# Two interleaved accumulation groups in place of two consecutive ones: the order of the map matmuls in a pre-activation directional convolution

## The chip, the cores and the metric

One Trainium2 chip, one of its cores. The metric is the device time of one execution in microseconds (us). The kernel before was run three times: median 2257.04 us, 2256.22 to 2261.09. The trace is of a further, profiled execution of it, which took 2258.2 us; its span, from the first instruction to the last, is 2256.4 us.

## The reference

The input x is 16 images of 256 channels of 56 by 56, float32. What is computed, cut to what matters:

```python
v = group_norm(x)                       # 32 groups of 8 channels, no affine part
h = depthwise_conv3x3(v, dw_weight)     # zero padding
h = gelu(h)
maps = einsum('bchw,oc->bohw', h, pw_weight) + pw_bias   # o: 8 directions x 256 channels
out = 0
for i, (dx, dy) in enumerate(OFFSETS8):
    out += maps[:, i] * (roll(v, (dy, dx)) - v)
return x + out
```

## The kernel before, in words

**Tiling.** An image is cut into seven tiles of eight rows, 448 pixels; 256 channels are two halves of 128 partitions. There are 112 tiles in all, in eight bodies of two images (14 tiles) each, every body written out by the same code; `n0 + nl` is the number of a tile and t its place in its image, 0 to 6. Eight directional maps of two channel halves are needed per tile. The kernel joins two directions to a pair (`PAIRS`), so a tile has eight units, u0 to u7, each of one pair (u divided by two) and one channel half (the remainder). A unit has two sides, one map of 128 by 448 each.

**TensorE.** `make_maps` (L897) makes one unit. Weights and h are split into a high and a low part, so one side is six matmuls of 448 columns that accumulate in one PSUM bank: high and low weights with the high part of h for both halves of the 256 inputs (four), then the high weights with the low part of h (two). A unit is thus 12 matmuls and a tile 96. Each matmul has weights of its own, loaded just ahead of it. The units rotate through three groups of two banks (`GROUPS`, L64), side 0 in the first bank and side 1 in the second; before the first matmul of a unit TensorE waits until VectorE has done with the unit that used the group last (L904, usually three units ago). At the end of a body the order of the groups is changed, so that u6 of tile 13 of a body waits for u4, two units ago. The last matmul of each side counts up `maps_s`.

**ScalarE.** `add_bias` (L584) waits for side 0 of a unit, scales and shifts it in place, then waits for side 1 and does the same. Its stream is in order, and between the units stand its other steps (L622 to L638): after u1 the GELU of tile nl+2 (L577) and the first tap of the convolution of step nl+3 (L567, or L563 in two halves), after u2 the high part of h (L582), after u7 the normalising of tile nl+4 (L548); measuring the next image's moments and copying its edges are placed behind units 3 to 6.

**VectorE.** In order (L852 to L891): the products of u0 and u1 with the field differences (L707, kept as the tile's sums), tap 0, the product of u2 (in place in its PSUM banks), tap 1, the addition of u2 to the sums (L729, which also frees the banks of u2), the product of u3, tap 2, the products of u4 to u7 with taps 3 to 7 between them. The eight taps (L787, or L778 in two halves) belong to the convolution three tiles ahead. `product` waits for both biased sides of its unit (L706), tap 0 for ScalarE's first tap. Where t is 2, the ten short steps of the group statistics (L643) are begun, one at a time between the others, and most of them fall in the tile with t = 3; in that tile the taps are in two halves too.

**GpSimd and the DMA queues.** GpSimd makes the field differences, the low part of h (L340) and three additions of products per tile (L371), and sends the sums with accumulating transfers on its own queue. The SyncE queue loads the images.

Of the kernel before, what the change touches and what calls it, by code (L numbers as in the profile page):

```python
# [5 lines left out]
def preact_directional_conv(nc, x, pw_t, pw_b, dw, out):  # L6
# [4 lines left out]
    P = 128  # L11
    B, C, H, W = x.shape
    HALVES = C // P
# [53 lines left out]
    def last_user(q):  # L67

        p = q - 1
        while GROUPS[p % UNITS_BODY] != GROUPS[q]:  # L70
            p -= 1
        return p
# [6 lines left out]
    with ctx:  # L79
        def sb(name, shape, dt=F32):  # L80
            return ctx.enter_context(nc.sbuf_tensor(name, shape, dt))

        def sem(name):
            return ctx.enter_context(nc.semaphore(name))
# [9 lines left out]
        hhi = sb("hhi", [P, H_SLOTS, 2, PX], F32R)  # L94
        hlo = sb("hlo", [P, H_SLOTS, 2, PX], F32R)
# [20 lines left out]
        w_hi = sb("w_hi", [P, HALVES, DIRS * C], F32R)  # L116
        w_lo = sb("w_lo", [P, HALVES, DIRS * C], F32R)
# [37 lines left out]
        def maps(q):  # L155
            b = 2 * GROUPS[q % UNITS_BODY]
            return psum[:, b:b + 2, 0:PX]

        def unit_map(u, side):

            k, g = divmod(u, HALVES)
            return PAIRS[k][side], g
# [21 lines left out]
        def h_part(h, t, nl, kk):  # L184


            base = nl - t
            if t == TILES - 1:
                return h[:, H_SLOT[base + SINGLE], kk, :]
            return h[:, H_SLOT[base + 2 * (t // 2) + kk], t % 2, :]  # L190
# [27 lines left out]
        hlo_s = sem("hlo_s")  # L218
        maps_s = sem("maps_s")
# [43 lines left out]
        def run(body):  # L263

            for i in range(BODIES):
                body(i * STEPS, i * 2, i == BODIES - 1)
# [628 lines left out]
        @block.tensor  # L895
        def _(pe):
            def make_maps(n0, nl, u):  # L897

                t, q = nl % TILES, nl * UNITS + u

                need = nl + (1 if t == TILES - 1 else 2)
                wanted = t % 2 == 0

                pe.wait_ge(prod_s, n0 * UNITS + (last_user(q) + 1 + PROD0))  # L904
                if u == 0 and wanted:
                    pe.wait_ge(hhi_s, n0 + need)
                for side in range(2):
                    d, g = unit_map(u, side)
                    col = d * C + g * P
                    steps = [(w, hhi, kk) for kk in range(HALVES) for w in (w_hi, w_lo)]  # L910
                    steps += [(w_hi, hlo, kk) for kk in range(HALVES)]
                    for s, (w, h, kk) in enumerate(steps):
                        if u == 0 and side == 0 and s == 2 * HALVES and wanted:
                            pe.wait_ge(hlo_s, n0 + need)
                        last = nc.tensor.matmul(maps(q)[:, side, :], w[:, kk, col:col + P], h_part(h, t, nl, kk),  # L915
                                                start=s == 0, stop=s == len(steps) - 1)
                    last.then_inc(maps_s, 1)

            pe.wait_ge(w_lo_s, 1)

            def body(n0, b0, last):
                for nl in range(STEPS):
                    for u in range(UNITS):
                        make_maps(n0, nl, u)

            run(body)
# [26 lines left out]
```

## Time and profile before

| | |
|---|---|
| median of three runs | 2257.04 us |
| profiled execution | 2258.2 us |
| its span | 2256.4 us, 28684 instructions |
| mean granted TensorE clock | 0.999 of full speed |
| first matmul starts | at 45.4 us |
| last matmul starts | at 2249.5 us |
| TensorE matmul busy | 2194.2 us, 10752 matmuls |
| VectorE busy | 2055.0 us |
| ScalarE busy | 1842.0 us |
| GpSimd busy | 1977.0 us |

The busy time of matmuls is that of overlapping instructions, merged: a row of 0.36 us stands for one matmul, though the next starts 0.20 us after it. The starts are therefore what is to be read of TensorE. Times in the timeline are from the start of the span; "[0.50 <-PE psum L915]" at the end of a row is idle time of that engine ahead of the row, and what ended it. "xN" in a timeline row is N instructions of one kind that follow each other, merged, and its second number is the time from the start of the first to the end of the last.

### The profile page before, as it was taken

To read this page: it belongs to the slowest core of one execution; us is meant where nothing else is said; L and a number is where in the kernel's file an instruction comes from. 1 tells how busy PE (TensorE), PEld (TensorE's weight loads), DVE (VectorE), ACT (ScalarE), POOL (GpSimd) and SP (SyncE) were. 2 spreads that over 40 slices of the span, in tenths; PEclk is the share of its full clock that TensorE was granted. 3 is DMA by queue.
4 is the path that set the end of the run, shared out by engine and by line. 5 is a ranking of instruction groups with operands and counts; after the bars stand their busy time and mean duration, and the time that the engine had idled before them with its cause. 6 is when DMAs were issued, how large, how long until landed. Compare 5 with 4: busy or idle time off the path is not lost.

```text
span 2256.4 us, 28684 instructions
## 1 busy us (share of the span) xinstructions
PE 2194.2 (97%) x10752; PEld 2009.3 (89%) x10752; DVE 2055.0 (91%) x2234; ACT 1842.0 (82%) x2762; POOL 1977.0 (88%) x857
## 2 busy tenths in 40 slices
PE   1999999999999999999999999999999999999998
PEld 1999989999999999999989999999999999999997
DVE  7999989999899999999989999899999999989995
ACT  5978888788887888889788887888878888787775
POOL 5889888899988998899898988989888998889985
PEclk9999999999999999999999999999999999999999
DMA  6245263443725337164452644526354372543414
GB/s 180 50 83 117 50 112 93 90 99 52 156 47 106 90 58 156 33 108 97 74 131 35 122 94 82 112 50 129 76 93 96 61 159 34 107 98 50 98 33 74
DMA packets 47083, 202.13 MB, mean 90 GB/s; under 512 B 3040, under 2 KB 7136, under 8 KB 45664
## 3 DMA queue, kind: packets, MB, share of 16 engines
q0 software_dynamic: 30192, 94.97, 25.8%
q1 hardware_dynamic: 16752, 105.34, 18.2%
q8 instruction: 84, 1.38, 0.2%
q14 instruction: 55, 0.45, 0.1%
HBM read 104.88 MB, written 146.80 MB: 112 GB/s over the span
## 4 chain that ended last, share of the span: by engine, by line
PE 89%; DVE 5%; ACT 4%; issue 2%; DMA 0%; POOL 0%; SPq 0%; ACTq 0%; DVEq 0%
PE psum L915 89%; DVE psum L707 1%; ACT psum L592 1%; DVE psum L787 1%; ACT hid L577 1%; ACT psum L563 1%; DVE acc L729 1%; DVE products L707 1%; DVE psum L778 1%; DMA acc<-x 0%; ACT psum L567 0%; DVE acc L759 0%; POOL hlo L340 0%; DVE fields L810 0%; DVE part_sums L797 0%
## 5 line engine op out<-in xcount | busy, mean ns | idle before, releaser
L592 ACT ACTIVATE psum<-psum,bias,rstd 128x448 f32<-128x448 f32 x1792 | 1203.7, 694 | 373.8 <-PE psum L915 369.7
L915 PE MATMUL psum<-hhi,w_hi 128*128 128x448 f32 x3584 | 1315.0, 367 | 55.4 <-ACT hhi L582 45.4
L371 POOL TENSOR_TENSOR acc<-acc,products 128x896 f32<-128x896 f32 x333 | 1165.1, 3499 | 231.4 <-DVE products L707 224.9
L915 PE MATMUL psum<-hhi,w_lo 128*128 128x448 f32 x3584 | 1305.3, 364 | 0.0
L915 PE MATMUL psum<-hlo,w_hi 128*128 128x448 f32 x3584 | 1014.1, 364 | 0.3 <-POOL hlo L340 0.3
L787 DVE SCALAR_TENSOR_TENSOR psum<-xn,dw_f,psum 128x896 f32<-128x896 f32 x768 | 881.2, 1148 | 79.8 <-ACT psum L567 76.3
L915 PEld LDWEIGHTS psum<-hhi,w_hi 128*128 128x128 f32 x3584 | 672.5, 188 | 137.8 <-issue 45.4
L915 PEld LDWEIGHTS psum<-hlo,w_hi 128*128 128x128 f32 x3584 | 672.5, 188 | 52.4 <-POOL hlo L340 0.9
L915 PEld LDWEIGHTS psum<-hhi,w_lo 128*128 128x128 f32 x3584 | 672.9, 188 | 50.0
L707 DVE TENSOR_TENSOR products<-psum,fields 128x896 f32<-128x896 f32 x555 | 600.9, 1083 | 37.9 <-ACT psum L592 35.6
L707 DVE TENSOR_TENSOR acc<-psum,fields 128x896 f32<-128x896 f32 x224 | 241.2, 1086 | 46.3 <-ACT psum L592 44.7
L340 POOL TENSOR_TENSOR hlo<-hid,hhi 128x896 fp32r<-128x896 f32 x112 | 264.6, 2363 | 12.7 <-ACT hhi L582 12.7
L356 POOL TENSOR_TENSOR fields<-xpad 128x896 f32<-128x896 f32 (+1 forms) x112 | 240.1, 2144 | 0.0
L352 POOL TENSOR_TENSOR fields<-xpad 128x912 f32<-128x912 f32 (+1 forms) x112 | 210.1, 1876 | 0.0
L778 DVE SCALAR_TENSOR_TENSOR psum<-xn,dw_f,psum 128x448 f32<-128x448 f32 x256 | 160.7, 677 | 6.5 <-ACT psum L563 6.5
L707 DVE TENSOR_TENSOR psum<-psum,fields 128x896 f32<-128x896 f32 x117 | 128.6, 1099 | 17.7 <-ACT psum L592 10.7
L378 POOL DMA_DIRECT2D out<-acc x111 | 132.7, 1196 | 7.8 <-DMA out<-acc 7.2
L729 DVE TENSOR_TENSOR acc<-psum,acc 128x896 f32<-128x896 f32 x111 | 120.1, 1082 | 0.2
L548 ACT ACTIVATE xn<-xpad,shift,rstd 128x1008 f32<-128x1008 f32 (+1 forms) x96 | 116.5, 1214 | 0.0
L577 ACT ACTIVATE hid<-psum 128x896 f32<-128x896 f32 x112 | 102.0, 911 | 12.0 <-DVE psum L787 12.0
L567 ACT ACTIVATE psum<-xn,dw_f 128x896 f32<-128x896 f32 x96 | 97.5, 1016 | 9.0 <-ACT hid L577 0.4
L582 ACT CAST hhi<-hid 128x896 fp32r<-128x896 f32 x112 | 104.8, 936 | 0.0
(67 smaller groups left out, 447.9 us busy)
## 6 DMA issues: line engine op xcount, KB each, us to landing
out<-acc POOLq DMA_DIRECT2D x96, 896.0 KB, 7.7
out<-x SPq DMA_DIRECT2D x16, 3136.0 KB, 12.9
xpad<-x SPq DMA_DIRECT2D x30, 1568.0 KB, 15.2
out<-acc POOLq DMA_DIRECT2D x15, 448.0 KB, 5.7
acc<-x SPq DMA_DIRECT2D x4, 784.0 KB, 6.9
xpad<-pw_t SPq DMA_DIRECT2D x1, 2048.0 KB, 12.3
out<-products SPq DMA_DIRECT2D x2, 224.0 KB, 1.9
dw_f<-dw SPq DMA_DIRECT2D x1, 9.0 KB, 8.2
```

The costliest lines, as they stand in the source:

```text
L340: nc.gpsimd.tensor_tensor(hlo[:, slot], hid[:], hhi[:, slot].bitcast(F32), ALU.subtract).then_inc(hlo_s, 1)
L352: nc.gpsimd.tensor_tensor(gx[:, :, f + 2 * lo:f + TR, :], v[:, :, r + 2 * lo:r + TR, 1:WP], v[:, :, r + 2 * lo:r + TR, 0:WP - 1], ALU.subt ...
L356: nc.gpsimd.tensor_tensor(gy[:, :, f + lo:f + ROWS + 1, :], v[:, :, r + lo + 1:r + TR, 1:W + 1], v[:, :, r + lo:r + ROWS + 1, 1:W + 1], AL ...
L371: nc.gpsimd.tensor_tensor(a, a, p, ALU.add).then_inc(added_s, 1)
L378: pool.dma_start(out_dst[b, :, :, t * PX:(t + width) * PX], acc[buf][:, :, sign].rearrange("p g t x -> p g (t x)"), accum_op=ALU.add).then ...
L577: nc.scalar.activation(hid[:], conv_of(n0, c), ACT.Gelu).then_inc(gelu_s, 1)
L592: nc.scalar.activation(m, m, ACT.Identity, bias=bias[ip][:, g, d:d + 1], scale=rstd[ip][:, g:g + 1]).then_inc(biased_s, 1)
L707: return nc.vector.tensor_tensor(to.rearrange("p s (r c) -> p s r c", c=W), maps(q).rearrange("p s (r c) -> p s r c", c=W), field, ALU.mult)
L729: nc.vector.tensor_tensor(a, maps(nl * UNITS + u), a, ALU.add).then_inc(prod_s, 1)
L778: nc.vector.scalar_tensor_tensor(d, xn[c % 2][:, g * TR + ky:g * TR + ky + ROWS, kx:kx + W], dw_f[:, g, TAPS_DVE[j]:TAPS_DVE[j] + 1], d, A ...
L787: nc.vector.scalar_tensor_tensor(d, xn[c % 2][:, ky:ky + 2 * ROWS, kx:kx + W].rearrange("p (a r) c -> p a r c", a=2), dw_f[:, g, TAPS_DVE[ ...
L915: last = nc.tensor.matmul(maps(q)[:, side, :], w[:, kk, col:col + P], h_part(h, t, nl, kk), start=s == 0, stop=s == len(steps) - 1)
```

## The change

For each unit, the loop over the six steps now stands outside and the loop over the two sides inside. Matmul s of side 0 is followed by matmul s of side 1, each into its own bank; the weights, the moving operands, the number of matmuls and of weight loads, the order of the units, the rotation of the groups and the wait ahead of a unit stay. The wait for the low part of h in u0 stands ahead of the first of the four matmuls that read it, so it now has eight matmuls before it and not four. The counts of `maps_s` come at the last two matmuls of the unit. No other engine's code is changed.

```diff
-                for side in range(2):
-                    d, g = unit_map(u, side)
-                    col = d * C + g * P
-                    steps = [(w, hhi, kk) for kk in range(HALVES) for w in (w_hi, w_lo)]
-                    steps += [(w_hi, hlo, kk) for kk in range(HALVES)]
-                    for s, (w, h, kk) in enumerate(steps):
-                        if u == 0 and side == 0 and s == 2 * HALVES and wanted:
-                            pe.wait_ge(hlo_s, n0 + need)
+                steps = [(w, hhi, kk) for kk in range(HALVES) for w in (w_hi, w_lo)]
+                steps += [(w_hi, hlo, kk) for kk in range(HALVES)]
+                for s, (w, h, kk) in enumerate(steps):
+                    if u == 0 and s == 2 * HALVES and wanted:
+                        pe.wait_ge(hlo_s, n0 + need)
+                    for side in range(2):
+                        d, g = unit_map(u, side)
+                        col = d * C + g * P
                         last = nc.tensor.matmul(maps(q)[:, side, :], w[:, kk, col:col + P], h_part(h, t, nl, kk),
                                                 start=s == 0, stop=s == len(steps) - 1)
-                    last.then_inc(maps_s, 1)
+                        if s == len(steps) - 1:
+                            last.then_inc(maps_s, 1)
```

## Rows read from the trace of the kernel before

**Rows 1.** The page: busy time (share of the span) and instructions of each engine.

```profile
PE 2194.2 (97%) x10752; PEld 2009.3 (89%) x10752; DVE 2055.0 (91%) x2234; ACT 1842.0 (82%) x2762; POOL 1977.0 (88%) x857
```

**Rows 2.** Who waited for whom: us in total, times, longest.

```profile
ACT psum L592 <- PE psum L915: 369.7, 711, 2.2
...
PEld psum L915 <- DVE acc L729: 33.4, 83, 0.8
...
PE psum L915 <- DVE acc L729: 6.1, 16, 0.5
...
PE psum L915 <- POOL hlo L340: 0.3, 1, 0.3
```

**Rows 3.** Timeline of TensorE's matmuls in one tile: start, us, instructions.

```profile
1094.38 0.56 PE L915 MATMUL psum<-hlo,w_hi 128*128 128x448 f32 x2
1094.78 0.36 PE L915 MATMUL psum<-hhi,w_hi 128*128 128x448 f32 x1
...
1101.58 0.56 PE L915 MATMUL psum<-hlo,w_hi 128*128 128x448 f32 x2
...
1102.09 0.48 PE L915 MATMUL psum<-hhi,w_hi 128*128 128x448 f32 x1
...
1102.40 0.37 PE L915 MATMUL psum<-hhi,w_lo 128*128 128x448 f32 x1
```

**Rows 4.** Timeline of ScalarE in the same stretch.

```profile
1094.98 0.70 ACT L592 ACTIVATE psum<-psum,bias,rstd 128x448 f32<-128x448 f32 x1 [0.50 <-PE psum L915]
1095.60 0.91 ACT L577 ACTIVATE hid<-psum 128x896 f32<-128x896 f32 x1
1096.61 1.02 ACT L567 ACTIVATE psum<-xn,dw_f 128x896 f32<-128x896 f32 x1
1097.56 1.30 ACT L592 ACTIVATE psum<-psum,bias,rstd 128x448 f32<-128x448 f32 x2
1098.78 0.94 ACT L582 CAST hhi<-hid 128x896 fp32r<-128x896 f32 x1
```

**Rows 5.** Timeline of VectorE in the same stretch.

```profile
1094.97 2.08 DVE L707 TENSOR_TENSOR acc<-psum,fields 128x896 f32<-128x896 f32 x2
1097.66 1.16 DVE L787 SCALAR_TENSOR_TENSOR psum<-xn,dw_f,psum 128x896 f32<-128x896 f32 x1 [0.60 <-ACT psum L567]
1098.89 1.10 DVE L707 TENSOR_TENSOR psum<-psum,fields 128x896 f32<-128x896 f32 x1
1099.90 1.15 DVE L787 SCALAR_TENSOR_TENSOR psum<-xn,dw_f,psum 128x896 f32<-128x896 f32 x1
1100.95 1.08 DVE L729 TENSOR_TENSOR acc<-psum,acc 128x896 f32<-128x896 f32 x1
```

**Rows 6.** Stretches of time: length, PE busy (matmuls), granted clock, DMA share, GB/s.

```profile
67.58:2190.46 2122.88, 2114.24 (x10369) 1.00 0.44 88
1089.98:1109.42 19.44, 19.44 (x97) 1.00 0.29 48
1169.27:1189.09 19.82, 19.82 (x97) 1.00 0.25 80
106.43:126.36 19.93, 19.48 (x98) 1.00 0.28 47
2034.22:2054.15 19.93, 19.48 (x98) 1.00 0.28 47
1679.92:1700.00 20.08, 19.70 (x98) 1.00 0.70 132
2190.46:2209.66 19.20, 19.20 (x97) 1.00 0.29 49
```

**Rows 7.** Timeline of TensorE behind two waits: the first and the last slow start.

```profile
138.77 0.36 PE L915 MATMUL psum<-hhi,w_lo 128*128 128x448 f32 x1
138.98 0.37 PE L915 MATMUL psum<-hhi,w_hi 128*128 128x448 f32 x1
...
1947.78 0.37 PE L915 MATMUL psum<-hhi,w_lo 128*128 128x448 f32 x1
1947.99 0.57 PE L915 MATMUL psum<-hlo,w_hi 128*128 128x448 f32 x2
```

**Rows 8.** Line L915: duration in ns, least, median and most, and first and last start.

```profile
L915 PEld LDWEIGHTS psum<-hhi,w_hi x3584: 186/188/330, 45.4 to 2248.7; 128*128 128x128 f32 x200
```

## The prediction

> **What bounds the kernel now.** The page's first part comes first: matmuls cover 97% of the span, and no other engine is above 91% [rows 1]. TensorE looks like the bound, but matmuls overlap, so I went on to the starts. From the first matmul of tile 1 to that of tile 109 are 2122.88 us, 108 tiles, 19.66 us a tile; one of the last tiles, where VectorE has no taps left to do, takes 19.20 us, which is 96 steps of 0.200 us [rows 6]. So a tile holds 0.46 us that the matmul stream alone doesn't need. The list of waits says where some of it goes: TensorE waits for the addition of u2 (L729) in 83 + 16 = 99 tiles [rows 2]. That wait is short, but its frequency is what matters: in 99 of 111 tiles the banks of u2 come free later than u5 would like to start. The timelines of one such tile show the path that decides it. Call M the start of the last matmul of u1's side 1, 1094.58 (the second of the pair at 1094.38) [rows 3]. ScalarE, idle for 0.50 us, starts the bias of that side 0.40 us later; behind it, without a gap, come GELU, the first tap and the two biases of u2, which end at 1098.86 [rows 4]. VectorE starts u2's product at 1098.89, then tap 1, then the addition, which ends at 1102.03 [rows 5], and u5 starts at 1102.09, M + 7.51 [rows 3]. TensorE would have been there at M + 37 steps = M + 7.40. From u5's start to the next M are 59 steps: the first takes 0.31 us [rows 3], the others 0.20, together 11.91. 7.51 + 11.91 = 19.42, the tile's 19.44 [rows 6]. The kernel is thus a loop over three engines: TensorE up to M, ScalarE and VectorE up to the addition, TensorE again. TensorE is not what it would be in a loop of its own, the bound with room behind it.
>
> **Part 1: the alternation of banks.** Twelve matmuls and twelve weight loads a unit stay. What alternation could bring is a shorter step. The old order changes bank at every sixth matmul, so the trace shows both kinds of step: the pair at 1094.38 ends one side, the next matmul at 1094.78 is the first in another bank [rows 3], 0.20 us after its predecessor, as inside a side. I take 0 for this part. Bounds: below, the step can't be shorter than the weight load of 0.188 us [rows 8], which is a gain of 0.012 us a step; above, TensorE has a slower gait in which a step is 0.2065 us (a tile of 19.82 us without a wait, against 19.20 [rows 6]), a loss of 0.0065. The row nearest to the new step is the change of bank itself, hence 0.
>
> **Part 2: when the sides are ready.** Before, side 0 is ready six steps ahead of side 1, and its bias is done by then. After, side 0's last matmul is one step (0.20 us) ahead of side 1's. ScalarE starts it at M + 0.20, and side 1's bias has to queue behind it. One bias occupies ScalarE for 0.62 us (1094.98 to 1095.60), two for 1.22 (1097.56 to 1098.78) [rows 4]. The work behind them starts at M + 0.20 + 1.22 = M + 1.42 and not at M + 1.02: 0.40 us later. Bounds: it can't be under 0.20 + 1.22 - 1.02 less a few hundredths, since ScalarE idles before u1's side 1 in the row and has no older work then; it could be larger only if the step became slow. Nothing is queued in the old gap that could move forward: ScalarE's stream is in order.
> What waits for that: GELU, first tap and u2's two biases follow back to back (u2's sides are ready at about M + 2.6 and M + 2.8, the biases start at M + 3.4), so all end 0.40 later, at M + 4.68. VectorE's tap 0 ends before that and has had 0.60 us of idle time ahead of it [rows 5]; the product of u1 (ends at M + 2.5, now at M + 2.6) still precedes it. Product, tap and addition of u2 move by 0.40; u5 starts at M + 7.91, 0.51 us behind TensorE's own pace. No slack takes the shift in, because the wait at u5 already exists in 99 tiles. A wait at u5 then delays all that follows, including the next M, and so costs its full length once a tile.
> Trainium skill, "Perfetto Trace Analysis", Matmuls: independent matmul groups should rotate through banks so that the evacuation of one overlaps the next group's matmuls. The trace agrees for the old order (side 0's bias runs under side 1's matmuls, ScalarE idles 0.50 us before the next); the rule speaks against this change, which lets both groups of a unit end together.
>
> **Part 3: the rest.** The wait for the low part of h moves from the fifth to the ninth matmul of u0; it cost 0.3 us once [rows 2], so nothing. The other bank waits (u0 to u4, u6, u7) have about 2 us of room: their products stand three units back with no such chain. The products of u5 and u6 get their biases 0.40 later, VectorE may idle some tenths there, and catches up in its idle time ahead of the next tap 0. ScalarE is at 82%, GpSimd at 88% [rows 1], and both have a longer tile to do the same. DMA issues hang on GpSimd's order, which is unchanged.
>
> **The gait.** TensorE steps at 0.200 or at 0.2065 us; it keeps one gait until a wait at u5 or u6, and behind it takes up one anew (in the first and the last slow start the step is 0.21 us from the third matmul on [rows 7]). I counted in the timeline 89 new starts behind a wait, 82 at u5 and 7 at u6; 19 of them slow, 15 and 4. Share 0.21. After the change nearly every tile has a wait (37 slow steps are 7.64, still under 7.91), so each tile draws a gait: a slow one adds 58 x 0.0065 = 0.38, in the mean 0.08.
>
> **The sum.** Of the 108 tiles, 16 have t = 3, with statistics steps and half taps in the path: 19.93 in the first and the last of them, 19.97 in the mean of the sixteen [rows 6]. The other 92 average (2122.88 - 16 x 19.97) / 92 = 19.60.
> - Ordinary tiles after: 7.91 + 11.91 + 0.08 = 19.90, less 19.60, is 0.30; x 92 = +28.
> - t = 3: 19.93 + 0.40 + 0.08 = 20.41, less 19.97; x 16 = +7.
> - The last tile of a body also waits at u6, as one of 20.08 against 19.44 does now [rows 6]: 0.64 x 7, which the mean of 19.60 holds but my 19.90 doesn't: +4.5.
> - Tile 0 and, in the last tile, its u6 wait and the last product: three times 0.40, +1.
> Together +41 us. The profiled execution took 2258.2, 1.2 above the median of the runs; 2258.2 + 41 = 2299, and against the median 2298.
>
> **Rivals.**
> - *The step gets shorter (faster).* If the 12 ns between weight load and step were the price of adding into the bank just written, alternation would remove them at 10 of 12 steps or all. Place: the 58 steps from u5 to M. Then a tile is 7.91 + 0.31 + 58 x 0.188 = 19.12, 0.78 less than forecast, 0.48 less than now in an ordinary tile and 0.35 in one with t = 3; with the last two lines of the sum about -44 us, 2214. It beats the 0.40 of part 2 as soon as a step falls by over 0.005 us or so (0.30 / 58). Against it: the change of bank in the old order costs and gains nothing. Chance 0.06. Beside it: the Trainium skill ("TensorE: Matmul & The Clock Gate", Back-to-back issue gap) gives N / 2.4 + 2.5 ns for the isolated step at full clock, an estimate of 189 ns for 448 columns; by it 11 ns of the present step are something else, which would speak for this rival, but it has no term for the bank, and the rows don't show its 189 anywhere.
> - *Cover (no change).* The shift of 0.40 falls into idle time; ScalarE waits for TensorE 369.7 us in all [rows 2]. Then 2257 to 2259. Against it: none of that idle time lies between M and the addition. Chance 0.05.
> - *Slow gait as a rule (slower still).* If the later release, or the alternation, makes most starts slow, the sum rises by up to 108 x 0.30 = 33: 2310 at half, 2331 at all. For it: I don't know what picks the gait. Chance 0.14.
>
> **How the numbers follow.** Forecast 0.75: 2298, with 2284 to 2308 as its own range (no slow start: 2290; a shift of 0.35: 2293; both, 2285). The range 2282 to 2314 takes in half of the slow rival. Within 0.2% (4.5 us, about what a measurement of this kernel can tell from no change): the cover, 0.05. Faster: 0.06. Slower: 0.89.
>
> **What would show it.** Right: u5 waits for L729 in about 108 tiles, 0.5 us each beyond the step; the first bias of u1 starts at M + 0.20 and GELU at M + 1.42; the addition ends at M + 7.86; fast tiles are 19.83 long. Part 1 is wrong if steps inside a unit are other than 0.200 or 0.2065. Wrong altogether if u5's wait stays near 0.1 us, or if another wait (u3 or u4 for the first products) appears.

## The result, and the profile after

The changed kernel takes 2298.3 us (median of four runs, 2296.54 to 2299.98); the kernel before takes 2257.5 us in the runs beside it. The ratio is 1.0179, 95% interval 1.0168 to 1.0191: slower, by 41 us. The profiled execution took 2299.98 us against 2258.2 before, 41.8 us more.

The page of the changed kernel, first the busy times (as in [rows 1]), then its chain of work that ended last, by engine:

```profile
PE 2198.8 (96%) x10752; PEld 2009.9 (87%) x10752; DVE 2059.8 (90%) x2234; ACT 1814.7 (79%) x2762; POOL 1976.0 (86%) x857
...
PE 59%; ACT 19%; DVE 14%; issue 7%; DMA 0%; ACTq 0%; SPq 0%; DVEq 0%
```

No engine has noticeably more to do (VectorE 4.8 us, ScalarE 27 us less). Before, the same chain was 89% TensorE, 5% VectorE and 4% ScalarE. Now a third of it runs through the other two, which is what a wait that ends late once a tile looks like.

Who waited for whom, as in [rows 2]: us in total, times, longest.

```profile
ACT psum L592 <- PE psum L917: 443.0, 446, 3.5
...
PEld psum L917 <- DVE acc L729: 83.3, 109, 1.2
...
PE psum L917 <- DVE acc L729: 40.8, 91, 0.9
...
PEld psum L917 <- DVE products L707: 7.7, 14, 0.7
```

The wait at u5 is in 109 tiles now. ScalarE waits for TensorE fewer times, 446 and not 711, because it waits once a unit and finds the second side ready. These rows also correct a reading of the prediction: 109 + 91 is more than 111 tiles, so the rows of the weight load and of the matmul count the same wait (each of the 91 stands beside one of the 109), and the two of before must not be added either. Before, 83 of 111 tiles had a wait at u5, not 99; that fits the 82 starts behind a wait at u5 that the prediction itself counts from tile 1 on.

The timeline of one tile with t = 4, as [rows 3, 4, 5] were: TensorE, ScalarE, VectorE. M, the last matmul of u1, is the fourth of the row at 1254.50, at 1255.10.

```profile
1254.50 0.96 PE L917 MATMUL psum<-hlo,w_hi 128*128 128x448 f32 x4
...
1263.03 0.67 PE L917 MATMUL psum<-hhi,w_hi 128*128 128x448 f32 x2 [0.37 <-DVE acc L729]
```

```profile
1255.30 1.31 ACT L592 ACTIVATE psum<-psum,bias,rstd 128x448 f32<-128x448 f32 x2 [1.04 <-PE psum L917]
1256.53 0.92 ACT L577 ACTIVATE hid<-psum 128x896 f32<-128x896 f32 x1
1257.54 1.02 ACT L567 ACTIVATE psum<-xn,dw_f 128x896 f32<-128x896 f32 x1
1258.50 1.29 ACT L592 ACTIVATE psum<-psum,bias,rstd 128x448 f32<-128x448 f32 x2
```

```profile
1259.82 1.10 DVE L707 TENSOR_TENSOR psum<-psum,fields 128x896 f32<-128x896 f32 x1
1260.83 1.15 DVE L787 SCALAR_TENSOR_TENSOR psum<-xn,dw_f,psum 128x896 f32<-128x896 f32 x1
1261.89 1.08 DVE L729 TENSOR_TENSOR acc<-psum,acc 128x896 f32<-128x896 f32 x1
```

| from M, us | before | forecast | after |
|---|---|---|---|
| GELU starts | 1.02 | 1.42 | 1.43 |
| biases of u2 start | 2.98 | 3.4 | 3.40 |
| product of u2 starts | 4.31 | 4.71 | 4.72 |
| addition of u2 ends | 7.45 | 7.86 | 7.87 |
| u5 starts | 7.51 | 7.91 | 7.93 |

Stretches, as in [rows 6]: the 108 tiles from tile 1 on, a fast ordinary tile, a slow one, one with t = 3, and the last tile of a body.

```profile
67.79:2231.46 2163.67, 2118.19 (x10370) 1.00 0.44 86
1250.50:1270.33 19.83, 19.46 (x97) 1.00 0.29 47
227.62:247.84 20.22, 20.09 (x97) 1.00 0.27 46
107.49:127.83 20.34, 19.47 (x98) 1.00 0.27 46
1710.90:1731.55 20.65, 19.93 (x97) 1.00 0.68 127
```

The 108 tiles took 2163.67 against 2122.88 us, 40.8 of the 41.8 us. A fast ordinary tile takes 19.83, where one of before took 19.44; a slow one 20.22.

### The profile page after: what moved, and what is told of

It reads as the page before. It is cut to its first block, busy times and chain, and to the rows that moved or that the text cites. A ratio compares the mean times of both kernels' runs of the same rounds, so it can differ in the third digit from the quotient of the medians.

```text
span 2298.2 us, 28684 instructions
## 1 busy us (share of the span) xinstructions
PE 2198.8 (96%) x10752; PEld 2009.9 (87%) x10752; DVE 2059.8 (90%) x2234; ACT 1814.7 (79%) x2762; POOL 1976.0 (86%) x857
## 4 chain that ended last, share of the span: by engine, by line
PE 59%; ACT 19%; DVE 14%; issue 7%; DMA 0%; ACTq 0%; SPq 0%; DVEq 0%
PE psum L917 59%; ACT psum L592 10%; DVE psum L707 5%; DVE acc L729 5%; ACT psum L567 4%; ACT hid L577 4%; DVE psum L787 1%; ACT psum L563 1%; DVE products L707 1%; DVE psum L778 1%; DMA acc<-x 0%; DVE acc L759 0%; ACTq L560 0%; DVE fields L810 0%; DVE part_sums L797 0%
## 5 line engine op out<-in xcount | busy, mean ns | idle before, releaser
L592 ACT ACTIVATE psum<-psum,bias,rstd 128x448 f32<-128x448 f32 x1792 | 1172.2, 691 | 443.3 <-PE psum L917 443.0
L917 PE MATMUL psum<-hhi,w_hi 128*128 128x448 f32 x3584 | 1026.3, 367 | 92.4 <-ACT hhi L582 45.1
L917 PE MATMUL psum<-hhi,w_lo 128*128 128x448 f32 x3584 | 1013.0, 364 | 0.0
L917 PE MATMUL psum<-hlo,w_hi 128*128 128x448 f32 x3584 | 866.3, 363 | 0.0
L917 PEld LDWEIGHTS psum<-hhi,w_hi 128*128 128x128 f32 x3584 | 663.6, 188 | 183.5 <-DVE acc L729 83.3
L729 DVE TENSOR_TENSOR acc<-psum,acc 128x896 f32<-128x896 f32 x111 | 120.1, 1082 | 0.2
```

The lines of the kernel that those rows point to most:

```text
L592: nc.scalar.activation(m, m, ACT.Identity, bias=bias[ip][:, g, d:d + 1], scale=rstd[ip][:, g:g + 1]).then_inc(biased_s, 1)
L729: nc.vector.tensor_tensor(a, maps(nl * UNITS + u), a, ALU.add).then_inc(prod_s, 1)
```

## The experiments

Two theories stand against each other. **Chain:** the whole price is that u1's side 1 gets its bias late, since everything between it and u2's addition is in series. **Alternation:** changing the bank at each matmul, or late biases in all units, costs a little everywhere. The first two kernels divide the change by units, the next two by how far side 0 is ahead. All four replace the fixed loop by a list `order` of (step, side).

**Only u1 interleaved; all but u1 interleaved.**

```diff
+                if u == 1:      # the other kernel: u != 1
+                    order = [(s, side) for s in range(n) for side in range(2)]
+                else:
+                    order = [(s, side) for side in range(2) for s in range(n)]
```

> Only u1 is interleaved; the other seven units keep the old order (side 0, then side 1). Chain theory (the price is the late bias of u1's side 1, which delays GELU, first tap, u2's biases and product, and the addition that u5 waits for): all of the price is here, u5 starts at M + 7.91, time 2293 to 2300 us, beside 2298.3 for the full change. Rival (alternation of banks or the late biases of many units cost a little everywhere): one eighth of 41 us, so about 2263.

Measured: 2295.3 us (2294.12 to 2296.49), 1.0173 of the kernel before (1.0149 to 1.0197).

> Seven units are interleaved, u1 keeps the old order. Chain theory: the bias of u1's side 1 starts at M + 0.40 again, u5 at M + 7.51, time 2256 to 2260 us, as the kernel before. Rival (price spread over the units): seven eighths of 41 us, about 2294.

Measured: 2261.1 us (2258.05 to 2264.89), 1.0023 (1.0011 to 1.0034). u5 starts at M + 7.92 with u1 alone interleaved and at M + 7.51 with all but u1 (medians of the tiles with t other than 3), as the chain theory has it. The waits for u2's addition, first with u1 alone interleaved, then with all but u1:

```profile
PEld psum L922 <- DVE acc L729: 85.8, 109, 1.2
```

```profile
PEld psum L922 <- DVE acc L729: 35.3, 90, 0.8
```

One unit of eight carries nearly all of the price. The other seven leave some 5 us (2261.1 against 2255.8 for the kernel before in the runs beside it), a little above what was expected. Part of it is in the trace: behind a body's last tile u0 of the next tile has a new wait, 0.19 to 0.27 us each with the step behind it, 1.5 us for the seven. A last tile without slow steps therefore takes 20.23 us from start to start, against 20.08 in [rows 6]. The rest can't be told from the changing share of slow steps (below): the two profiled executions lie only 0.5 us apart (2258.69 and 2258.2).

**Side 0 ahead by two steps, by three.** In all units most steps alternate banks, but the last two or three of side 0 stand ahead of the last two or three of side 1.

```diff
+                lead = 2        # the other kernel: 3
+                order = [(s, side) for s in range(n - lead) for side in range(2)]
+                order += [(s, side) for side in range(2) for s in range(n - lead, n)]
```

> All units alternate banks, but side 0 ends two steps ahead of side 1 and not one. Chain theory: the second bias queues for 0.61 - 2 x 0.20 = 0.21 us and not 0.41; u5 starts at M + 7.72; ordinary tiles 7.72 + 11.91 + 0.06 = 19.69, the sum about +17 us: 2270 to 2279. Rival (alternation costs): still 2298, since nearly all steps alternate.

Measured: 2273.9 us (2271.47 to 2274.6), 1.0075 (1.0046 to 1.0103).

> As the kernel with a lead of two steps, but with three: the first seven steps of a unit alternate, then side 0 ends, then side 1. Chain theory: 0.61 - 0.60 = 0.01 us of queueing is left, u5 at M + 7.52, 2256 to 2262 us, though most steps still alternate. Rival (alternation costs): about half or more of the 41 us stays, 2278 or above.

Measured: 2251.8 us (2249.3 to 2253.72), 0.9982 (0.9971 to 0.9993).

ScalarE behind M in the same tile of both, M being 1241.57 with a lead of two and 1230.59 with three:

```profile
1241.57 1.31 ACT L592 ACTIVATE psum<-psum,bias,rstd 128x448 f32<-128x448 f32 x2 [1.04 <-PE psum L921]
1242.81 0.92 ACT L577 ACTIVATE hid<-psum 128x896 f32<-128x896 f32 x1
```

```profile
1230.39 1.31 ACT L592 ACTIVATE psum<-psum,bias,rstd 128x448 f32<-128x448 f32 x2 [1.04 <-PE psum L921]
1231.62 0.92 ACT L577 ACTIVATE hid<-psum 128x896 f32<-128x896 f32 x1
```

GELU starts at M + 1.43 with a lead of one step, M + 1.24 with two, M + 1.03 with three and M + 1.02 with the old six: what queues is one bias's time on ScalarE less the lead. u5 follows at M + 7.92, 7.72, 7.53 and 7.51 (medians of the tiles with t other than 3), and so do the times, 2298, 2274, 2252, 2257. With three steps of lead eight of a unit's twelve steps still change the bank (two in the old order), the step stays at 0.200 us, and a fast ordinary tile takes 19.43 or 19.44 us in nearly all cases (19.41 to 19.45 before): alternation as such costs nothing here.

The kernel with three steps of lead is even 4 us faster than the kernel before (2251.8 against 2255.8 in the runs beside it), and below the 2256 to 2262 that I expected. Its trace doesn't put that down to the order of the matmuls: it has 1507 slow steps where that of the kernel before has 2992, which is 10 us, while its waits are 4 us longer. Whether the order has a part in the slow steps no run shows.

**A shorter chain.** If the chain is what binds, taking work out of it should free both orders. ScalarE's first tap moves behind u2's biases, VectorE's tap 0 behind u2's product, tap 1 behind the addition (it stands behind u3's product, ahead of tap 2). The work is the same, only its order changes.

```diff
-        GELU_AT, START_AT, HHI_AT, NORM_AT = 1, 1, 2, 7
+        GELU_AT, START_AT, HHI_AT, NORM_AT = 1, 2, 2, 7
...
                     first_product(n0, nl, 1)
+                    second_product(n0, nl)
                     tap_next()
                     stats_next()
-                    second_product(n0, nl)
                     stats_next()
-                    tap_next()
                     stats_next()
                     second_add(n0, nl)
...
                     kept_product(n0, nl, 3)
                     stats_next()
+                    tap_next()
                     tap_next()
```

> Old matmul order, shorter chain: ScalarE's first tap stands behind u2's biases and VectorE's tap 0 behind u2's product, tap 1 behind the addition. Chain theory: u2's biases end at M + 3.5, the addition at M + 6.6 (M + 7.1 where t is 3), before TensorE needs the banks at M + 7.4, so the waits at u5 go. Then TensorE runs at its own step: 112 x 19.2 us is 2150 and the time 2213 us if the step is 0.200, up to 2283 if it is 0.2067 throughout; 2210 to 2240 expected. Rival (the shares of ScalarE and VectorE bound the kernel, not this order): 2250 or more with waits elsewhere.

Measured: 2251.8 us (2244.48 to 2270.99 in ten runs), 0.9999 (0.997 to 1.0027). No gain, and above what was expected. Two stretches of one tile each, both without any wait, show the first half of the reason:

```profile
1161.94:1181.14 19.20, 19.20 (x97) 1.00 0.27 85
711.58:731.42 19.84, 19.84 (x98) 1.00 0.74 137
```

The wait at u5 did go, but for a short one in 15 tiles with t = 3 (row below), and TensorE then ran over six tiles, 611 steps and more, from one wait to the next at its own step; but where that step was the slow one, it stayed slow for as long. Counted by the starts, 3221 of its 10751 steps were slow (0.203 to 0.215 us; longer ones are waits), about 21 us. The other half is waits that I had not listed: u6 in a body's last tile now stands 1.0 to 1.2 us, because u4's product is behind two taps and u5 no longer holds TensorE back, and u2 behind a tile with t = 3 waits for u7's product, 0.4 us in ten of fifteen cases.

```profile
PEld psum L915 <- DVE acc L729: 4.1, 15, 0.3
```

> The interleaved order with the same shorter chain. Chain theory: the biases of u2 end at M + 3.9, the addition at M + 7.0, still before M + 7.4; interleaving costs nothing here or a few us where t is 3 (M + 7.5): within 10 us of the kernel with the old order and the short chain, given the same share of slow steps. Rival (interleaving has a price of its own): 41 us above that kernel.

Measured: 2256.2 us (2246.34 to 2261.75), 0.9996 (0.9978 to 1.0015). The interleaved order is within 5 us of the old one here, as expected, and not 41 us above. A part of the price stays, though, which the share of slow steps hides: in the traces the old order has 3221 slow steps and the interleaved one 2509, 5 us less, while its waits are 14 us longer. Of these 6 us are at u5 in the tiles with t = 3, where the addition still comes too late. The waits of the weight load for it:

```profile
PEld psum L917 <- DVE acc L729: 10.5, 15, 0.7
```

**The other waits out as well.** VectorE's stream once more, against that of the short chain: u4's and u7's products one tap earlier, the statistics steps behind u2's addition.

```diff
                     second_product(n0, nl)
                     tap_next()
-                    stats_next()
-                    stats_next()
-                    stats_next()
                     second_add(n0, nl)
-                    stats_next()
+                    for _ in range(4):
+                        stats_next()
                     kept_product(n0, nl, 3)
                     stats_next()
                     tap_next()
-                    tap_next()
                     stats_next()
                     kept_product(n0, nl, 4)
                     tap_next()
+                    tap_next()
                     kept_product(n0, nl, 5)
...
+                    kept_product(n0, nl, 7)
                     tap_next()
                     stats_next()
-                    kept_product(n0, nl, 7)
                     tap_next()
```

> The old matmul order and the short chain, with VectorE's stream arranged so that hardly any wait of TensorE is left: statistics steps behind u2's addition, u4's product one tap earlier (for the wait at u6 in a body's last tile), u7's product one tap earlier (for the wait at u2 behind the tile with t = 3). Theory that the slow step is drawn at a wait and kept until the next: few draws, so single runs lie apart, near 2212 us where the step of 0.200 is kept, up to 2280 where the slow one is; median most likely 2212 to 2230. Rival (the slow step comes and goes with something other than waits, such as the load on PSUM or SBUF): about 28% slow steps as before, 2230 to 2240, with the change of step seen far from any wait.

Measured with the old matmul order: 2221.6 us (2220.94 to 2228.97), 0.9844 of the kernel before (0.9827 to 0.9861). This is the fastest version, 1.6% below the kernel before and 77 us below the changed one. Its stretch from tile 1 to tile 109 (before: 2122.88 [rows 6]) and what is left of TensorE's waits on VectorE:

```profile
67.23:2154.00 2086.77, 2081.96 (x10370) 1.00 0.44 89
```

```profile
PEld psum L913 <- DVE acc L707: 9.1, 15, 0.6
...
PEld psum L913 <- DVE products L707: 5.3, 14, 0.6
```

The tile's mean is 19.32 us, against 19.20 for 96 steps of 0.200. L729 is no longer among what TensorE waits for: the addition ends at M + 6.68, and u5 starts at M + 7.40. Only 147 steps were slow in this profile.

> The same with the interleaved order. Chain theory: u2's addition ends at M + 7.0, in time for u5, so the median lies within the scatter of the kernel with the old order and the same VectorE stream, at most 10 us above. Rival (a price of the interleaving itself): 41 us above.

Measured with the interleaved order: 2239.6 us (2238.04 to 2240.79), 0.9914 (0.9898 to 0.9931), 18 us above the kernel before it, not the 10 at most that I expected. The addition ends at M + 7.10 and u5 starts at M + 7.40, so the chain at u5 is not what costs. The profile has 1858 slow steps, 1711 more, which is 11 us; the other 8 us are waits at u0 and u3 around the tile with t = 3 and at u6 in a body's last tile. So with all else out of the way the later side 0 costs something again. Why the slow steps are more is not shown: 6 of 56 starts behind a wait were slow, against 4 of 44 in the old order, hardly a difference; but the slow step was kept for up to 634 steps, and there for 35 at most.

## Why the prediction was right

It forecast 2298 and 2298.3 was measured. (The four terms of its sum are 40.5 us, rounded up to 41; the profiled executions lie 41.8 us apart.) By its steps:

- **What bounds the kernel** was read rightly: a loop over three engines that closes at u5, although the busy share and the chain of the page point at TensorE. The count of 99 tiles was wrong (83, see above); no term rested on it, since the sum was made from the mean tile.
- **Part 1, alternation costs or gains nothing:** right. The steps stay at 0.200 and 0.2065 us, and the kernel with three steps of lead shows no price at the bank changes.
- **Part 2, 0.40 us a tile:** measured 0.41 to 0.42 from M, and 0.39 from a fast tile of before (19.44) to one after (19.83). Each time from M in the table is within 0.02 us of the forecast, and the kernel with u1 alone interleaved shows that the place is right too.
- **Part 3, nothing elsewhere:** nearly. Behind a body's last tile u0 now waits about 0.26 us (seven times, 1.8 us), which I had not seen. The prediction gave u0 to u4, u6 and u7 "about 2 us of room" and showed no row for it. In the trace of before most have 1.1 to 2.9 us between the work that frees their banks and their start, u2 in and behind a tile with t = 3 has 0.8 to 0.9, and u0 of a body's first tile only 0.30 to 0.39, since the changed order of the groups makes it wait for u6, two units back. That is less than the 0.40 by which the biases come later. The waits of the weight load for these products were 7 before (row below), all at u6, and are 14 now. The two kernels that divide the change by units put the other seven units at some 5 us at most.

```profile
PEld psum L915 <- DVE products L707: 5.1, 7, 0.7
```

- **The step:** I took 21% of slow starts. Counted after, 17 of 115 at u5 and u6, and 4 of 7 at the new wait at u0, 17% together. The slow steps fell from 2992 to 1792 of 10751 with about as many slow starts (19 and 21), because each is now ended by the next wait. The total came out right partly because this and the waits at u0 nearly cancel, which is luck: ordinary tiles have a mean of 19.97 us, where 19.90 + 4.5 / 92 = 19.95 was forecast, and those with t = 3 20.38, where it was 20.41.
- **The rivals:** the shorter step and the cover are out by the timeline; a slow step as the rule did not come.

## What to carry to other kernels

Where an engine is busy 97% of the span and yet waits briefly at the same place in most rounds, the round is a loop through other engines, and a delay anywhere in its serial part is paid in full, each round. Ask of a reordering when each result becomes ready, not only how much work there is: two results that end together make their reader, one in-order engine, serve them one behind the other. And look at what else stands in the streams between the two ends of the loop: with ScalarE's first tap and one of VectorE's two taps moved out of it, and with the waits that came next moved as well, the interleaved order went from 2298.3 to 2239.6 us and the old one from 2258.0 to 2221.6. The first move alone brought the old order nothing.

## What the runs showed of the hardware

At a granted clock of 0.999 TensorE has two steps for the same pair of weight load and matmul, 0.200 and 0.2065 us. It keeps one of them over six tiles and more without a wait (19.20 and 19.84 us a tile, the two stretches above) and usually changes it where a wait holds up the weight load. The wait can be too short to lengthen a step: in the last kernel the slow step begins at u5 of tile 108, where one weight load starts 0.08 us late. The first step behind the start after a wait takes 0.31 us and not 0.20.

Of the starts behind a wait 21% were slow in the kernel before and 17% in the changed one, but 9% with u1 alone interleaved and 30% (11 of 37) in the old order with the short chain. This moves single runs: the last-named kernel spread over 26 us in ten runs. Few waits do not mean few slow steps, since a slow step also lasts longer then: with 37 such starts that kernel had 3221 slow steps, the fastest version with 44 had 147, the one with u1 alone interleaved with 115 had 963. What picks the step is open. The addition that frees the banks of u5 ends at the same time from M in fast and slow cases (7.868 and 7.870 us in the changed kernel, medians). The places may not be random: in the old order with the short chain the slow starts at u2 are those of tiles 25, 53 and 81 and of 32, 60 and 88, 28 tiles apart. One trace of each kernel can't tell, and no run was made to settle it.
